# A ring of five buffers in place of three for the third layer's outputs, in the stage that finishes a graph network

## The reference, cut to what matters

```
for l in range(3):
    h = x @ W[l].T
    agg = segment_sum(h[src] * norm[:, None], dst, N) + b[l]
    x = relu(gamma[l] * (agg - mean(agg)) * rsqrt(var(agg) + eps) + beta[l])
x = layernorm(x_in + x)
x = layernorm(x + messages(x, src, dst, edge_attr_20, edge_weight, edge_attr_3))
```

## Time and profile before

| | |
|---|---|
| three runs | 1647.95, 1646.83 and 1639.43 us, median 1646.83 |
| the profiled execution | 1645.93 us |
| its span, first to last instruction | 1644.2 us |
| granted clock of TensorE over the span | 0.897 |
| `finish_gcn` in it | about 1123 to 1360 us |

### The profile page before, as it was taken

The page is one execution under the profiler, slowest core; times in us unless marked ns, Lnnn a source line. Parts: engine busy times, 40 slices in busy tenths (PEclk is TensorE's granted clock), DMA queues, the critical chain, the costliest instruction groups (busy, mean ns, idle before and its releaser), DMA issues. The chain is left out here.

```text
span 1644.2 us, 24535 instructions
## 1 busy us (share of the span) xinstructions
PE 1315.3 (80%) x7509; PEld 1116.2 (68%) x7509; DVE 1119.7 (68%) x3189; ACT 904.1 (55%) x1789; POOL 903.5 (55%) x788
## 2 busy tenths in 40 slices
PE   4774799999989799999997999995544426999981
PEld 3664688878877688888876888884433325777760
DVE  7558466655656586767947878785887755677772
ACT  3760344433434576767664766654656673566663
POOL 5773677777774677878735243320333333356655
PEclk7997799999999799999998999997676667999995
DMA  2001988787867667677655666643998853355644
GB/s 65 2 2 35 305 271 278 252 266 256 274 221 258 226 220 249 239 265 264 221 201 168 209 212 228 237 157 83 356 341 330 318 212 80 70 107 127 136 95 106
DMA packets 132502, 326.48 MB, mean 199 GB/s; under 512 B 34356, under 2 KB 66764, under 8 KB 129556
## 3 DMA queue, kind: packets, MB, share of 16 engines
q1 hardware_dynamic: 79796, 181.78, 31.8%
q0 software_dynamic: 52576, 143.13, 29.1%
HBM read 164.31 MB, written 165.08 MB: 200 GB/s over the span
## 5 line engine op out<-in xcount | busy, mean ns | idle before, releaser
L1070 PE MATMUL ps_b<-yhi,whi 128*128 128x492 f32 (+1 forms) x960 | 395.9, 412 | 19.3 <-ACT area L962 14.7
L1070 PE MATMUL ps_b<-yhi,wlo 128*128 128x492 f32 (+1 forms) x960 | 379.5, 395 | 0.0
L1070 PE MATMUL ps_b<-ylo,whi 128*128 128x492 f32 (+1 forms) x960 | 378.0, 394 | 0.0
L962 ACT COPY area<-ps_b 128x492 f32<-128x492 f32 (+1 forms) x240 | 137.9, 574 | 310.1 <-PE ps_b L1070 308.7
L880 DVE BATCH_NORM_STATS2 stat<-area 128x6 f32<-128x492 f32 (+1 forms) x240 | 161.9, 677 | 147.7 <-ACT area L962 147.4
L722 POOL DMA_INDIRECT rows<-area,node_at x160 | 180.5, 1128 | 111.3 <-ACT area L968 64.7
L1070 PEld LDWEIGHTS ps_b<-yhi,whi 128*128 128x128 f32 x960 | 185.4, 193 | 51.2 <-ACT area L962 15.1
L1070 PEld LDWEIGHTS ps_b<-yhi,wlo 128*128 128x128 f32 x960 | 183.6, 191 | 37.8
L1070 PEld LDWEIGHTS ps_b<-ylo,whi 128*128 128x128 f32 x960 | 185.0, 193 | 31.4 <-issue 0.5
L1216 POOL DMA_INDIRECT out<-fin_out,node_at x80 | 79.2, 990 | 179.0 <-DVE fin_out L1285 153.1
L729 POOL TENSOR_TENSOR area<-area,own_row 128x1016 f32<-128x1016 f32 x40 | 96.4, 2412 | 131.3 <-ACT area L946 131.0
(11 more groups left out here) (420 smaller groups left out, 2936.2 us busy)
## 6 DMA issues: line engine op xcount, KB each, us to landing
z<-area SPq DMA_DIRECT2D x30, 984.0 KB
area<-z SPq DMA_DIRECT2D x30, 984.0 KB, 8.3
z<-area SPq DMA_DIRECT2D x28, 1016.0 KB
area<-z SPq DMA_DIRECT2D x28, 1016.0 KB, 8.9
x_rows<-R SPq DMA_DIRECT2D x40, 256.0 KB, 4.2
x_rows<-area SPq DMA_DIRECT2D x40, 256.0 KB, 3.1
area<-x_rows SPq DMA_DIRECT2D x10, 1024.0 KB, 8.5
fin_xr<-x_rows SPq DMA_DIRECT2D x10, 1024.0 KB, 6.8
```

Source lines behind the costliest of these rows:

```text
L962: nc.scalar.copy(f.aggT[t % 2][:, j, 0:cols(t)], f.ps_b[j % 2][:, 0:cols(t)]).then_inc(x["copied"], 1)
L1070: o = nc.tensor.matmul(f.ps_b[j % 2][:, 0:n], w[:, c, j * P:(j + 1) * P], y[g % 2][:, c, 0:n], start=(c == 0 and i == 0), stop=(c == C - 1 ...
```

## The change: what it does

The ring for z has five buffers, X[0] to X[4]: position o uses X[(o + 3) % 5], so that positions 0 and 1 still find their blocks in X[3] and X[4], and the buffers of these two come into the ring when they are transposed. There are two semaphores more for the landings. In iteration b SP now issues z of b+2 in place of z of b, behind the same wait on PE; in iteration 4 it issues those of 5 and 6, behind the transposing of positions 0 and 1. No instruction is added to or taken from any other engine.

```diff
-    z_got, x_in = k.z_got, k.x_in + [m.sem(f"fin_x_in{i}") for i in range(2)]
+    z_got = [m.sem(f"fin_z_got{i}") for i in range(2)] + k.z_got
+    x_in = k.x_in + [m.sem(f"fin_x_in{i}") for i in range(2)]
...
     def z_at(o):
-        return f.X[3 + o] if o < 2 else f.X[(o - 2) % 3]
+        return f.X[(o + 3) % 5]
...
             for b in range(4, NB):
-                if b >= 5:
-                    sp.wait_ge(x["turned"], 4 * (b - 2))
-                    sp.dma_start(z_at(b)[:, :, 0:cols(b)], z_in[order[b], :, :, 0:cols(b)]).then_inc(z_got[(b - 2) % 3], 16)
+                for o in ((5, 6) if b == 4 else (b + 2,)):
+                    if o < NB:
+                        sp.wait_ge(x["turned"], 4 * (o - 4))
+                        sp.dma_start(z_at(o)[:, :, 0:cols(o)], z_in[order[o], :, :, 0:cols(o)]).then_inc(z_got[o % 5], 16)
                 sp.wait_ge(x["normed"], 4 * (b - 3))
                 sp.dma_start(f.xr[b % 4][:], x_rows[order[b]]).then_inc(x_in[b % 4], 16)
...
                     if b >= 2:
-                        act.wait_ge(z_got[(b - 2) % 3], 16 * ((b - 2) // 3 + 1))
+                        act.wait_ge(z_got[b % 5], 16 * (b // 5 + (1 if b % 5 >= 2 else 0)))
```

## The result

The changed kernel took 1624.32 us at the median of six runs (1619.69 to 1631.60), the kernel before 1645.64 (1639.43 to 1654.28). The ratio is 0.9873, 95% interval 0.9851 to 0.9896: 21 us faster. The prediction was 1628.8 us, range 1623 to 1639.

A forecast was written before the change was run, and what follows sets the result against it. From 1199 us the prediction saw a loop of late z loads holding ACT, and DVE through the root. Gains of 17.5 + 2.5 less 2.0 us for transfers made 18.0 us: 1628.8 us, range 1623 to 1639.

The forecast's parts named there:

- The bound and the loop: From 1199 us, late z delays ReLU, root and rows, hence SP's next z request; a round takes 21.56 us per pair.
- The six waits, 17.5 us: DVE's six waits at L1273 for ACT's root L1313 in the steady pairs would go, saving 17.5 us.
- The 2.5 us before the output's scaling: DVE's 12 short waits at L1285 for ACT's normalised E-block rows would all go, saving 2.5 us.
- a DVE pair of 18.1 us: Steady pair of turns on DVE once the 17.5 and 2.5 us of waits go: 18.1 us.
- The loss to the transfers, 2.0 us: In the steady pairs, faster pace needs 401 GB/s; 2 us of the gain taken as lost to transfers.
- The early start: Loads 5 and 6 issued between 1123 and 1152 us empty the queue by 2 MB; gain nothing by itself.
- The first rival: In the steady pairs transfers become the bound, leaving a gain of 5 to 14 us; chance 0.22.
- The second rival: In the steady pairs late xr makes DVE wait, up to 12 us slower at 20 us landings; slower given 0.04.
- the sign that it was wrong: Loads of xr landing later than 15 us after their issue would show the prediction wrong.
- The third: DVE's idle 17.5 us is set by something other than z, so time stays at 1646.8 us; chance 0.06.

The follow-up runs named there:

- the repeat: The changed kernel, unaltered, run again on the same chip beside the version with the scaling on ACT: 1624.18 us, 0.9905 of the kernel before.
- the late start: Changed kernel with z loads of positions 5 and 6 issued in iteration 5 together with position 7's: 1627.86 us, 0.9894 of the kernel before.

## Why the prediction was right

**The bound and the loop.** Right. The changed order on ACT with three buffers and the five buffers with the old lead tell apart what was claimed: it is the work behind a late ReLU that cost DVE its time, and the lead that cures it, not the buffers. That DVE lost it at the root is read from its waits; no run moves the root without the normalised rows.

**The six waits, 17.5 us.** Right: none is left.

**The 2.5 us before the output's scaling.** Right as to the wait, but the four instructions also got shorter, which the step left out. The grouped lines of the six pairs, before and then after (count, busy us, mean ns, idle us):

```profile
L1285 DVE TENSOR_SCALAR fin_out<-fin_x,fin_rstd 128x512 f32<-128x512 f32 x24 | 12.2, 508 | 2.7 <-ACT fin_x L1325 2.5
```

```profile
L1287 DVE TENSOR_SCALAR fin_out<-fin_x,fin_rstd 128x512 f32<-128x512 f32 x24 | 10.0, 482 | 0.0
```

That is 2.2 us of busy time less. About 0.6 us of it is the time of each one, 482 ns in place of 508. The rest is overlap: when the four run in a row, the records of neighbours overlap, and 24 x 482 ns = 11.6 us stand in 10.0 us; one by one behind ACT they did not overlap. The size could have been had beforehand, as the earlier trace rows show four in a row in 1.67 us, and four behind ACT took 12.2 / 6 = 2.03. The six pairs before, from the first L1247 to the last, with the columns of rows 2:

```profile
1198.83:1327.48 128.65, 57.18 (x258) 47.91 (x258) 98.00 (x289) 77.69 (x128) 47.93 (x50) 0.66 0.85 324
```

DVE's busy time in them fell by 98.00 - 94.90 = 3.1 us in all for the same 289 instructions, which no term of the sum held. The other 0.9 us is not traced to a line. The step "a DVE pair of 18.1 us" should have been 17.6.

**The loss to the transfers, 2.0 us.** Mis-sized for the first profiled execution: there it was nothing, a pair at 411 GB/s with no wait of DVE on a landing, and with a seventh of a pair's bytes taken away the time did not move. In the repeat it was 2.7 us of waits on xr, near the 2 us taken. Which of the two is usual, two profiles do not tell. The claim that being late "has first to use up a margin" holds.

With these two the sum comes out for the first profile: 17.5 + 2.5 + 3.1 + 0.1 (waits on PE) = 23.2 us, and the six pairs gave back 128.65 - 105.50 = 23.15 us. The whole span fell by 22.7, as the stage began 2.2 us later and the rest, ahead of the pairs and behind them, made up some 1.8. Both mis-sized terms made the forecast too slow, so the median lies near the lower end of the range. The medians differ by 21.3, and those of the repeat by 18.4.

**The early start.** "Nothing by itself" is not contradicted by the times. The trace of the late start shows 2.5 us of wait on the xr that stood behind three loads of z in a row, which no term of the prediction held. That SP's two waits more would cost nothing held.

**The first rival**, transfers as the bound, did not come about, but only just. By the 358 GB/s of HBM Reference in the Trainium skill, section Specifications (TRN2), a pair would have taken an estimated 20.3 us; the trace has 17.53 us at 411 GB/s. That agrees with the same section's remark that a core streaming alone gets more: this program runs on one core.

**The second rival**, xr late, was sized well for the first profile. The xr issued at 1222.06 was used at 1236.33, 14.3 us later (14.7 was forecast), and the longest landing of the steady part was 12.7: a margin of 1.6 (1.5 was forecast). Where landings went to 16.2 and 17.1, DVE did wait on xr, in the version with the scaling on ACT and in the repeat. The prediction named landings of xr beyond 15 us as the sign that it was wrong. That sign came in the repeat, at 17.1 us, and the gain stayed, since only the last two pairs were late, by 2.7 us together; the sign was drawn too tight. No xr landed as late as the 18.0 us from which it would have taken the whole gain. **The third**, that nothing moves, is out.

## What to carry to other kernels

Where an engine's in-order list holds an instruction that waits for a load, ask what stands behind it that needs nothing of the load; a wait that costs the bound engine can be cured by asking for the load earlier or by moving that other work ahead, and here each alone gave the same within the scatter. A buffer more is worth only the lead that it permits, so compare the lead with the longest landing under the traffic that the faster kernel will make. After such a gain, work out the traffic of the new pace at once: here DVE and the transfers then stood within a few per cent of each other, and taking work from DVE alone showed no clear gain.

## What the runs showed of the hardware that was not expected

The same program's loads of xr, 1 MB each, landed after 12.7 us at the longest in one execution and after 17.1 in another, at a slightly lower rate of all transfers (379 against 388 GB/s over the 100 us from 1200), so a margin of 1.6 us read from one trace is none. Reads and writes together went at 411 GB/s over a whole pair. The mean granted clock of PE in the six pairs rose from 0.66 to 0.76 of full speed (its two levels are 1.2 and 2.4 GHz, and a mean between them is a mixture), while PE was busy 57.18 of 128.65 us before and 51.18 of 105.50 after, with the same 258 matmuls; no run here shows why it rose. DVE's waits on PE stayed at 7.2 to 7.3 us all the same, so by way of these waits the higher clock gave no more than 0.1 us of the 23.15.
